# Second attention layer: row maxima computed twelve steps ahead of the scores, their row placed by products and a ScalarE copy

## The reference, cut to what matters

```python
x = x + L0(_gn(x)); x = x + L1(_gn(x))
q, k, v = split(x @ qkv_w.T + qkv_b)             # 12 heads of 32, N = 2304 tokens per image
attn = einsum('bqd,bkd->bqk', q * scale, k)
attn = attn + rel_h[:, :, :, :, None] + rel_w[:, :, :, None, :]
attn = softmax(attn, axis=-1)                    # 12 heads x 2 images, 2304 x 2304 each
out = einsum('bqk,bkd->bqd', attn, v) @ proj_w.T + proj_b
```

## Time and profile before

| | us |
|---|---|
| median of three runs | 3379.78 |
| lowest and highest | 3377.91, 3383.99 |
| the profiled execution, its own time | 3383.73 |
| its span in the profile | 3381.4 |
| first maximum matmul of `attention_full` | at 1246.28 |
| first scores matmul of `attention_full` | at 1311.94 |
| last clearing matmul L1592 of `attention_full` | at 3265.2 |

### The profile page before, as it was taken

One profiled execution on the slowest core, in us unless ns is written; L12 is line 12 of the kernel. 1 busy time (PEld: TensorE's weight loads), 2 busy tenths in 40 slices (PEclk: granted clock), 3 DMA queues, 4 the chain that ended last, 5 costly groups with the idle time before them and its releaser, 6 DMA issues. The chain is left out here.

```text
span 3381.4 us, 95017 instructions
## 1 busy us (share of the span) xinstructions
PE 2934.7 (87%) x33912; PEld 1907.3 (56%) x33912; DVE 2583.6 (76%) x5459; ACT 1802.1 (53%) x3290; POOL 1923.9 (57%) x1560
## 2 busy tenths in 40 slices
PE   1987999987298848999999999999999999999977
PEld 1554777764154623666566666666656666666644
DVE  6745888866763648988898888898989888889824
ACT  3333667664333512565555656555556565555664
POOL 3453555550303003777777777777777777777772
PEclk9997999998599557999999999999999999999989
DMA  2425655547032984222222222222222222222114
GB/s 114 187 85 134 144 131 142 143 106 259 31 135 68 240 174 130 49 49 49 50 49 50 49 50 49 50 49 50 49 50 49 50 49 50 49 50 49 40 44 140
DMA packets 165484, 295.05 MB, mean 87 GB/s; under 512 B 81546, under 2 KB 115428, under 8 KB 159588
## 3 DMA queue, kind: packets, MB, share of 16 engines
q1 hardware_dynamic: 165076, 289.54, 33.7%
HBM read 189.37 MB, written 85.45 MB: 81 GB/s over the span
## 5 line engine op out<-in xcount | busy, mean ns | idle before, releaser
L1700 POOL TENSOR_TENSOR fprob_low<-fprob 128x768 f16<-128x768 f32 x1008 | 1470.8, 1476 | 570.6 <-ACT fprob L1670 558.8
L1711 DVE TENSOR_REDUCE fpart_max<-fmax_acc 128x1 f32<-128x384 f32 x2592 | 1347.2, 553 | 169.7 <-PE fmax_acc L1552 156.2
L1670 ACT ACTIVATE fprob<-fscores 128x768 f32<-128x768 f32 x1296 | 1031.9, 806 | 769.1 <-PE fscores L1576 768.7
L1552 PE MATMUL fmax_acc<-fk_m,fq_m 128*128 128x384 f16 x2592 | 867.8, 336 | 132.8 <-DVE fpart_max L1711 82.9
L1574 PE MATMUL fscores<-fq_a,fk_a 128*128 128x384 f16 x2592 | 849.7, 328 | 36.2 <-issue 32.2
L1576 PE MATMUL fscores<-fq_b,fk_b 97*128 97x384 f16 x2592 | 853.1, 329 | 0.0
L1600 PE MATMUL fout_acc<-fv,fprob 128*128 128x65 f16 x7776 | 613.7, 191 | 8.2 <-POOL fprob_low L1700 6.6
L1601 PE MATMUL fout_acc<-fv,fprob_low 128*128 128x33 f16 x7776 | 597.2, 179 | 0.0
L1600 PEld LDWEIGHTS fout_acc<-fv,fprob 128*128 128x128 bf16 x7776 | 542.7, 97 | 73.4 <-POOL fprob_low L1700 23.2
L1601 PEld LDWEIGHTS fout_acc<-fv,fprob_low 128*128 128x128 f16 x7776 | 489.3, 96 | 53.5 <-issue 3.4
L1552 PEld LDWEIGHTS fmax_acc<-fk_m,fq_m 128*128 128x128 f16 x2592 | 252.5, 97 | 377.1 <-DVE fpart_max L1711 281.0
(11 more groups left out here) (128 smaller groups left out, 3823.7 us busy)
## 6 DMA issues: line engine op xcount, KB each, us to landing
q_a<-q_hi SPq DMA_DIRECT2D x48, 432.0 KB, 5.8
fq_a<-q_hi SPq DMA_DIRECT2D x48, 432.0 KB, 7.8
q_a<-q_lo SPq DMA_DIRECT2D x24, 432.0 KB, 7.4
row_bias<-x SPq DMA_DIRECT2D x24, 432.0 KB, 7.6
col_bias<-x SPq DMA_DIRECT2D x72, 144.0 KB, 3.8
fq_a<-q_lo SPq DMA_DIRECT2D x24, 432.0 KB, 8.4
fq_a<-col_bias SPq DMA_DIRECT2D x24, 432.0 KB, 12.0
fq_b<-row_bias SPq DMA_DIRECT2D x24, 432.0 KB, 14.8
```

The source lines that it names most:

```text
L1552: nc.tensor.matmul(max_acc[:, bank, 0:PIECE], q_m[:, b, tile * 128:(tile + 1) * 128], k_m[:, b, piece * PIECE:(piece + 1) * PIECE], start= ...
L1670: nc.scalar.activation(prob[:, k % RING, :].rearrange("p (j n) -> p j n", j=2), scores[:, 2 * (k % 2):2 * (k % 2) + 2, 0:UNIT], ACT.Exp).t ...
L1700: engine.tensor_tensor(prob_low[:, k % RING, :], prob[:, k % RING, :], prob[:, k % RING, :].bitcast(BF16)[:, 1::2], ALU.subtract).then_inc ...
L1711: nc.vector.reduce_max(part_max[:, j // PIECES, j % PIECES:j % PIECES + 1], max_acc[:, bank, 0:PIECE], axis=AX.X).then_inc(bank_read, 1)
```

## The change

- The maxima run 12 steps ahead (`AHEAD = PAIRS + 3`) and no longer 54: the prologue has 24 pieces and one row product; the last twelve steps of the last stage have no pieces, its other 42 do.
- The last piece of a unit is reduced in step 5 of the list. One DVE reduction with `negate=True` writes the negated maxima straight into column 96 of `neg_max`, now 128 x 3 x 128 in f16 and cleared once by POOL. `part_max` has two buffers. `tile_max`, the separate negation and `take_row` are gone.
- In step 7 (`ROW_STEP = 7`) PE runs three products of 128 columns with the identity, right behind the scores, in the bank that the next unit's piece j = 0 has left; their row 96 holds the maxima of 384 queries. ACT copies that row from PSUM into row 96 of `q_b` (1 x 384) behind the exponential of step 7. The rows' DMAs are gone.
- Banks: the next unit's j = 2 (the a piece of step 7) waits for j = 1, which stands just ahead of it, and j = 3 (the b piece of step 7) waits for ACT's copy.
- `normalise` stands behind the exponential of step 3 instead of that of step 2.
- SP issues `load_max` ahead of `load_main` in each stage, both for the next stage; the second stage's `load_max` is no longer in the prologue.

Its core:

```diff
-    LATE = NA - 1
+    AHEAD = PAIRS + 3
+    ROW_STEP = 7
...
+    def ahead(n, k):
+        m = k + AHEAD
+        if m < STEPS:
+            return n, m
+        return None if is_last(n) else (n + 1, m - STEPS)
+
+    def piece_bank(g, u, j):
+        if isinstance(g, int) and g == 0:
+            return j % 2
+        return (u + j + (1 if j < 2 else 0)) % 2
...
-            load_max(0, 1)
             max_consts(1, consts_in)
-            place_rows(0, 0, False)
...
                     if not is_first(n):
                         sp.wait_ge(prob_used, n * STEPS)
+                    load_max(h + b, 1 - b)
                     load_main(h + b, 1 - b)
...
+            def max_piece(n, b, m, part):
+                u, j = m // PAIRS, m % PAIRS * STEP_PIECES + part
+                g = n * NA + u
+                behind_row = not (isinstance(g, int) and g == 0)
+                if behind_row and j == 3:
+                    pe.wait_ge(row_copied, g)
+                elif behind_row and j == 2:
+                    pe.wait_ge(bank_read, g * UNIT_PIECES + 2)
+                elif due(g * UNIT_PIECES + j - 1):
+                    pe.wait_ge(bank_read, g * UNIT_PIECES + j - 1)
...
+            def row_of_max(n, u):
+                g = n * NA + u
+                pe.wait_ge(neg_ready, g + 1)
...
+                    pe.wait_ge(bank_read, (g + 1) * UNIT_PIECES + 1)
+                for t in range(QT):
+                    last = nc.tensor.matmul(max_acc[:, u % 2, t * 128:(t + 1) * 128], neg_max[:, t, :], ident[:, :],
+                                            start=True, stop=True)
+                last.then_inc(row_ready, 1)
...
-                if k == 0 and a in (0, LATE):
-                    pe.wait_ge(rows_in[a == LATE], ROWS * (n + 1))
+                if k == 0:
+                    pe.wait_ge(row_copied, n * NA + a + 1)
...
-            for u in range(NA):
-                for k in range(PAIRS):
-                    if u > 0 and k == ROW_STEP:
-                        row_of_max(0, u - 1)
-                    for part in range(STEP_PIECES):
-                        max_piece(0, 0, (u * PAIRS + k) * STEP_PIECES + part)
+            for m in range(AHEAD):
+                if m - AHEAD + PAIRS == ROW_STEP:
+                    row_of_max(0, 0)
+                for part in range(STEP_PIECES):
+                    max_piece(0, 0, m, part)
...
+            def place_row(n, u, b):
+                act.wait_ge(row_ready, n * NA + u + 1)
+                nc.scalar.activation(q_b[M_ROW:M_ROW + 1, b, u * UNIT:(u + 1) * UNIT],
+                                     max_acc[M_ROW:M_ROW + 1, u % 2, 0:UNIT], ACT.Identity).then_inc(row_copied, 1)
...
                     exps(n, k)
-
+                    coming = row_after(n, k)
+                    if coming:
+                        place_row(*coming, b if coming[1] else 1 - b)
...
-                    if rest == 0:
+                    if rest == 1:
...
+                if m % PAIRS == PAIRS - 1:
+                    dve.wait_ge(bank_read, (g + 1) * UNIT_PIECES)
+                    if due(g):
+                        dve.wait_ge(row_ready, g)
+                    nc.vector.reduce_max(neg_max[:, :, M_ROW:M_ROW + 1], part_max[:, u % 2], axis=AX.X,
+                                         negate=True).then_inc(neg_ready, 1)
```

More of the change, by code:

```diff
@@ L1407, in attention_full @@
     bank_read = sem("fbank_read")
-    tile_max_ready = sem("ftile_max_ready")
+    neg_clear = sem("fneg_clear")
     neg_ready = sem("fneg_ready")
-    rows_in = [sem(f"frows_in_{i}") for i in range(2)]
+    row_ready = sem("frow_ready")
+    row_copied = sem("frow_copied")
     lo_copied = sem("flo_copied")
@@ L1421, in attention_full, with row_after @@
     RESULT = 16
[L1422 to L1438, removed]
+    def ahead(n, k):
[7 more added lines that the diff above has]
+        return (u + j + (1 if j < 2 else 0)) % 2
+    def row_after(n, k):
+        unit = k // PAIRS + 1
+        if k % PAIRS != ROW_STEP or (is_last(n) and unit == NA):
+            return None
+        return (n, unit) if unit < NA else (n + 1, 0)
     def lows(n, p):
@@ L1496, in store @@
                 sp.dma_start(dst, result[:, b]).then_inc(result_out[b], 16)
[L1498 to L1506, removed]
             load_max(0, 0)
@@ L1522, in stage @@
                 n = h * B + b
[L1523 to L1527, removed]
                 if not is_last(n):
@@ L1545, in _ @@
         def _(pe):
[L1546 to L1552, removed]
+            def max_piece(n, b, m, part):
[8 more added lines that the diff above has]
+                    pe.wait_ge(bank_read, g * UNIT_PIECES + j - 1)
+                tile, piece = u * QT + j // PIECES, j % PIECES
+                nc.tensor.matmul(max_acc[:, piece_bank(g, u, j), 0:PIECE], q_m[:, b, tile * 128:(tile + 1) * 128],
@@ L1553, in max_piece @@
                                  k_m[:, b, piece * PIECE:(piece + 1) * PIECE],
                                  start=True, stop=True).then_inc(bank_filled, 1)
[L1556 to L1562, removed]
+            def row_of_max(n, u):
+                g = n * NA + u
+                pe.wait_ge(neg_ready, g + 1)
+                if isinstance(g, int) and g == UNITS - 1:
+                    pe.wait_ge(bank_read, g * UNIT_PIECES + UNIT_PIECES - 1)
+                else:
+                    pe.wait_ge(bank_read, (g + 1) * UNIT_PIECES + 1)
[3 more added lines that the diff above has]
+                last.then_inc(row_ready, 1)
@@ L1616, in stage @@
                 pe.wait_ge(main_in[b], (h + 1) * MAIN)
-                if not is_last(n):
-                    pe.wait_ge(max_in[1 - b], (h + 1 + b) * MAX)
                 for k in range(STEPS):
                     scores_of(n, b, k)
[L1621 to L1627, removed]
+                    coming = row_after(n, k)
+                    if coming:
+                        row_of_max(*coming)
+                    if k + AHEAD == STEPS and not is_last(n):
+                        pe.wait_ge(max_in[1 - b], (h + 1 + b) * MAX)
+                    later = ahead(n, k)
+                    side = b if k + AHEAD < STEPS else 1 - b
+                    if later:
+                        max_piece(later[0], side, later[1], 0)
                     if k >= LAG:
@@ L1631, in stage @@
                         weighted(n - 1, 1 - b, k - LAG + STEPS)
-                    if not is_last(n):
-                        max_piece(n + 1, 1 - b, k * STEP_PIECES + 1)
+                    if later:
+                        max_piece(later[0], side, later[1], 1)
             pe.wait_ge(consts_in, CONSTS)
@@ L1705, in _, with maxima @@
         def _(dve):
[L1706 to L1727, removed]
+            def maxima(n, m):
+                u = m // PAIRS
+                g = n * NA + u
+                for j in range(m % PAIRS * STEP_PIECES, (m % PAIRS + 1) * STEP_PIECES):
+                    dve.wait_ge(bank_filled, g * UNIT_PIECES + j + 1)
+                    nc.vector.reduce_max(part_max[:, u % 2, j // PIECES, j % PIECES:j % PIECES + 1],
+                                         max_acc[:, piece_bank(g, u, j), 0:PIECE], axis=AX.X).then_inc(bank_read, 1)
+                if m % PAIRS == PAIRS - 1:
[4 more added lines that the diff above has]
+                                         negate=True).then_inc(neg_ready, 1)
             def add_parts(n, a):
@@ L1739, in add_parts @@
                                         ALU.add).then_inc(sum_ready, 1)
[L1741 to L1746, removed]
+            dve.wait_ge(neg_clear, 1)
+            for m in range(AHEAD):
+                maxima(0, m)
             def stage(h, b):
@@ L1754, in stage @@
                         low_part(nc.vector, n - 1, STEPS - 1, low_by_dve)
[L1755 to L1763, removed]
+                    later = ahead(n, k)
+                    if later:
+                        maxima(*later)
                     u, rest = divmod(k - 1 - LAG, PAIRS)
@@ L1777, in _ @@
         def _(pool):
+            nc.gpsimd.memset(neg_max[:, :, :], 0.0).then_inc(neg_clear, 1)
             nc.gpsimd.memset(zeros[:, :], 0.0).then_inc(zeros_ready, 1)
```

16 lines of the change are left out of this document (6 added, 10 removed).

## The result

| | before | after |
|---|---|---|
| median | 3381.32 us (4 runs) | 3359.87 us (4 runs) |
| lowest and highest | 3377.91, 3383.99 | 3358.13, 3361.86 |
| the profiled execution, its own time | 3383.73 | 3359.43 |
| its span | 3381.4 | 3357.2 |

The ratio is 0.9932, with a 95% interval of 0.9917 to 0.9947: faster by 0.68%, 22 us between the medians. The direction was forecast, and 3359.87 lies inside the range of 3285 to 3365, but the forecast gain was 50 us, more than twice what came.

What follows compares the result with a forecast made beforehand. Bound: PE and DVE waiting for each other in full stages, PE and DVE sharing one job in the prologue. Prologue -50, last stage +8.3, full stages -8.3 sum to -50: 3333.7 us for the profiled execution, median 3330, range 3285 to 3365.

Steps and rivals of the forecast that it cites:

- What bounds the kernel: Full stages: neither PE nor DVE alone; a 13.35 us unit holds about 12.0 of PE work and some 1.36 of stalls.
- Removed stalls: Full unit: a(5)'s 0.68 us stall falls to 0.16, 0.24 and 0.28 go, the 0.18 behind low(7) stays at 0.19.
- So step 7 is 0.94 us longer: Each full unit: b(7) waits for ACT's copy, starting at e(7) + 1.25 instead of e(7) + 0.31; bounds 0.85 to 1.05.
- the next instruction starts about 0.70 later: ACT in step 7: the row's copy starts about 0.70 us after exp(7) starts, read from two exponentials taking 1.49.
- the term for the full stages: 138 units at 13.29 us instead of 13.35: -8.3 us, range -35 to +21.
- lands 4.4 us later, about 1262: Prologue: the last constant, issued after SP's queue frees at 1257.0, lands about 1262, when first scores start; prologue -50 us.
- rival D: Prologue: first scores wait for data, so its gain is absent; at most a few us; sign: after 1266; 2%.
- the queue was free at 1257: Prologue, argument against D: inputs issued by 1242 and queue free at 1257, so at most a few us at stake.
- Last stage: 42 of its 54 steps now carry pieces, so units there cost more: +8.3 us.
- Rival A: Full units: low(3) and low(7) meet POOL's low parts, up to 0.61 us more each; 14.5 a unit, 3501 in all; 7%.
- Rival B: Full units: stalls do not add up, 0.16 and 0.19 vanish, copy takes less; 12.75 us a unit, 3253 in all; 12%.
- Rival C: Steps behind the new wait cost 0.3 to 0.4 us a unit more, cancelling the prologue's gain; 3373 to 3387; 6%.

## Why the prediction was right and wrong, step by step

The forecast for the profiled execution was 3333.7 and it took 3359.4. Of these 26 us, 15 are the new wait of step 7, put too small, 7 are the constants that land late, and 4 are scatter. The two steps that failed are named below in the prediction's words.

**What bounds the kernel: right.** The stalls came one after another as they were read. The largest of the old ones was `normalise`, shown by moving that line alone: 0.51 of the 0.68.

**Removed stalls: right.** The residue at a(5) was forecast at 0.16 and is 0.18 (the step of 1.50 from 5 to 6). The one behind low(7) was forecast at 0.19 and is 0.18. The other two are gone. The row products were put at 0.055 each and take 0.17 for three. POOL holds up nobody: weighted(2) runs without a wait.

**"So step 7 is 0.94 us longer": the mechanism right, the term too small by 0.15.** It measured 2.41 - 1.32 = 1.09. What failed in it is "the next instruction starts about 0.70 later". That pitch came from two exponentials in a row. The row's copy starts 0.84 after the exponential, when this has ended. The copy's own 0.48 and PE's 0.06 were exact. With this the unit is 13.40 and not 13.29, and 138 units times 0.11 are 15 us: the term for the full stages was -8.3 and came out at +6.9. This is the larger part of the miss. That the wait is on the path at its full length was shown from both sides: 0.36 more a unit with a copy added, 0.67 less with the copy first, where 0.24 of the wait is left, and 0.92 less with the product inside the scores as well. By its own list PE would have begun b(7) at 2051.10, 0.91 before it did.

**"lands 4.4 us later, about 1262": wrong, 7 us.** The row gave the median from issue to landing for a group of two, one issued early and one at the end of a queue. The last constant lands 10 us or more after its issue. PE was done when forecast (1262), and what was late next was named, but its time was not. This is close to rival D, which was given 2% and "a few us at most". Its sign, first scores after 1266, did show (1270.01), though most of the prologue's gain came; its wording, that the first scores wait for data, is what happened to 8 of the 50 us. That "the queue was free at 1257" told when SyncE had issued, not when the data had landed. That x1's transfer was to blame was the first explanation and fell, and so did the one that laid it on the last constant alone. What holds is that all awaited constants stand behind the 97 packets of `in_one_b`, which go one at a time and took 9.1 us; that reading comes from the traces, not from a run with this load changed.

**Last stage: right**, +8.3 against +8.0.

**Rival A (DVE's low parts meet POOL's)** did not come. All 274 of them between 1270 and 3160 take 0.95, low(3) included; only in the last stage, where they fall into POOL's runs, does one take up to 1.56. By the rule of the Trainium skill ("SBUF — State Buffer", Who interferes with whom) a meeting would have made it wait; in full units there is none, so they neither support nor test it. **Rival B (12.75 a unit)** is the number reached when the copy goes first, 12.73, but by luck and not by its mechanism: the residue of 0.18 at a(5) is still there in that run, and in the changed kernel the catching up of the other engines saved nothing. **Rival C** in part: the unit did cost more than the walk, 0.11 and not 0.3, and for none of the reasons that it names.

The rest of the difference, +1.3 ahead of the layer and +2.8 behind it, is scatter as far as the other runs show.

## What to carry to other kernels

A gain from moving work ahead can be eaten up where the same edit puts a hand-over between two engines behind a long instruction. Look at what stands in the consumer's list directly ahead of the new instruction: here, one swap of two lines on ScalarE was worth some 83 us, more than the whole change. When a change has several parts, time each alone: one moved line was worth three times the total. Before shortening a stretch, ask for the last landing of what it covers, not for a group's median, and look in the transfers' view for a load whose packets go one at a time. And multiply the saving of a median unit only by units that look like it.

## What was not expected of the hardware

ScalarE starts an instruction 0.68 to 0.71 us after the start of an exponential that lasts 0.81, for another exponential, for `take_lo`, for `normalise` and for a 128 x 384 copy. It starts the 1 x 384 copy to partition 96 only at 0.84, behind the exponential's end, and the exponential behind that copy only 0.51 after it, a copy of 0.48. In the first layer the copies of 1 x 384 and 32 x 384 stand alike 0.5 apart. The other surprise is the tail of the transfers: 6 us and more at 18 to 37 GB/s, where 328 GB/s stand in the first slice of the second of those rows. It is one load of 169.8 KB on 97 partitions, whose packets follow each other singly for 7.6 us even with nothing issued behind it.
